# Second layer of an edge network: half of its features in three fp32r products, half in fp32, with a new order of VectorE's and ScalarE's units

## The chip, the cores and the metric

The kernel runs on one core of a Trainium2 chip. The metric is the device time of one execution in microseconds (us). TensorE multiplies, VectorE (DVE), ScalarE (ACT) and GpSimd (POOL) work on tiles, and SyncE (SP) issues plain DMAs. The engines run side by side and order themselves by semaphores alone. In the profile PE is TensorE's matmul and PEld its weight load.

## The reference

```python
h = jnp.maximum(_layernorm(x, axis=-1), 0.0)               # x: 6250 x 256
polarity = jnp.clip(edge_attr[:, 0:1], 0.0, 1.0)           # 206250 edges, sorted by dst
raw = edge_attr[:, 1:]                                     # 64 features
e = jax.nn.relu(raw @ W_e1.T + b_e1) @ W_e2.T + b_e2       # 256 hidden, 256 out
edge_emb = (e * (polarity + 0.01)) @ W_le.T + b_le
msg = jax.nn.relu(h[src] + edge_emb)
aggr = jax.ops.segment_sum(msg, dst, num_segments=6250)
h2 = (h + aggr) @ W_g1.T + b_g1                            # then layer norm, relu, @ W_g2.T + b_g2
out = x + (relu(ln(h2)) @ W_g2.T + b_g2)
```

`W_e2` and `W_le` are multiplied into one 256 x 256 matrix (`wc`) on the chip, since the gate is one number per edge. So an edge costs two layers: 64 to 256 with a ReLU, then 256 to 256.

## The kernel before

The edges are cut into 403 units of 512, each of four blocks of 128. One window of at most 128 nodes takes the messages of seven units (58 windows); the 49 node tiles are brought to their end in between, spread over the units of later windows. A unit u goes through these steps, and each engine runs its own loop over u, in the order written in its block:

- GpSimd gathers the rows of h for the four blocks (L577), at most four units ahead of `total` and three ahead of the second layer.
- ScalarE rounds the raw features to fp32r (`raw_high`, L422) and VectorE computes the rest that rounding lost (`raw_low`, L427). TensorE's `first_layer` (L798, L799) makes two fp32r products for each half k of the hidden features, into the PSUM banks LA[0] and LA[1].
- ScalarE's `hidden_high` (L588) writes relu of both halves to `hh` in fp32, which frees LA for the next unit.
- ScalarE's `seed` (L593) puts the constant c2 in the four LB banks, two a unit. `second_layer` (L820) adds, for each block, two fp32 products of 256 columns. Each fp32 product shows as two records of the profile, so 16 a unit.
- VectorE's `total` (L675) computes gate * LB + gathered row, once a block, ScalarE's `message_high` (L600) rounds its relu to fp32r, and VectorE's `message_low` (L685) computes what is left.
- VectorE's `onehot` (L664) compares slots with an iota; `segment` (L836) multiplies the one-hot rows by high and low parts side by side (512 columns), summing a window in the bank SG[g % 2]: left half the high parts, right half the low.
- After the window's last unit ScalarE's `window_out` (L608) copies all 512 columns to `agw`, TensorE's `window_turn` (L844) transposes and adds both halves by four fp32 products with the identity (eight records), and VectorE's `window_add` (L699) adds the result to `aggT`.

The loops before the change run per unit: TensorE second_layer(u), first_layer(u+2), segment(u-1), then window and node work. ScalarE hidden_high(u+1), lift, raw_high(u+3), seed(u+1), two message_high(u), window_out. VectorE node steps and total(u), message_low(u), raw_low(u+3), onehot(u+1), more node steps. The node steps are `up` (L855, L856), `stats` (L704), `moments` (L708), `invert` (L712), `norm` (L718), `turn` (L863), `lift` (L621), `down` (L869, L870) and `finish` (L725).

Of the kernel before, what the change touches and what calls it, by code (L numbers as in the profile page):

```python
# [4 lines left out]
F32 = mybir.dt.float32  # L5
# [8 lines left out]
D = 256  # L14
# [12 lines left out]
GU = 7  # L27
# [23 lines left out]
def gnn(nc, x, src, dst, src_m, dst_m, pol_m, pol, first, attrT, attr_m, W_e1T, b_e1, b_e1r, W_e2, b_e2, W_leT, b_le,  # L51
        W_g1T, b_g1, ln_g, ln_b, W_g2T, b_g2, out):
    ctx = ExitStack()
    with ctx:
# [15 lines left out]
        w1r = sb("w1r", [P, 2, D], F32R)  # L70
        c2r = sb("c2r", [P, D], F32R)
# [22 lines left out]
        def setup(c):  # L94
# [90 lines left out]
            def vector(eng):  # L185
# [18 lines left out]
                link(eng, eng.tensor_copy(c2r[0:1, :], c2[0:1, :]))  # L204
                eng.tensor_tensor(c2r[32:33, :], c2[0:1, :], c2r[0:1, :].bitcast(F32),
# [259 lines left out]
        def edge_path():  # L465
            with ExitStack() as c:
# [6 lines left out]
                hh = sb("hh", [P, 2, 2, 512], F32, c)  # L473
# [3 lines left out]
                agw = sb("agw", [P, 2 * D], F32, c)  # L477
# [4 lines left out]
                r_hh = sem("r_hh", c)  # L482
                r_l2 = sem("r_l2", c)
# [6 lines left out]
                r_ev = sem("r_ev", c)  # L490
                n_x = [sem(f"n_x{i}", c) for i in range(NXT)]
# [90 lines left out]
                def _(eng):  # L582
                    def hidden_high(u):
                        if u >= 2:
                            eng.wait_ge(r_l2, 2 * (u - 2) + 2)
                        for k in range(2):
                            eng.wait_ge(r_l1, 2 * u + k + 1)
                            eng.activation(hh[:, u % 2, k, :], LA[k][:, :], ACT.Relu).then_inc(r_hh, 1)  # L588
# [15 lines left out]
                    def window_out(g):  # L604
                        eng.wait_ge(r_sg, min(GU * g + GU, UNITS))
                        if g >= 1:
                            eng.wait_ge(r_tr, g)
                        eng.copy(agw[:, :], SG[g % 2][:, :]).then_inc(r_ev, 1)  # L608
# [26 lines left out]
                    for u in range(UNITS):  # L635
                        if u + 1 < UNITS:
                            hidden_high(u + 1)
# [3 lines left out]
                        if u + 3 < UNITS:  # L641
                            raw_high(eng, u + 3)
# [17 lines left out]
                def _(eng):  # L660
                    def onehot(u):
# [18 lines left out]
                    def message_low(u):  # L680
                        if u >= 2:
                            eng.wait_ge(r_sg, u - 1)
                        for q in range(2):
# [5 lines left out]
                                                     op0=ALU.max, op1=ALU.subtract).then_inc(r_ml, 1)  # L689

# [52 lines left out]
                    raw_low(eng, 2)  # L743
                    eng.wait_ge(s_sl, 1)
                    onehot(0)
                    for u in range(UNITS):
                        t = TILE_AFTER.get(u // GU - 1)
                        if u % GU == 4 and t is not None:
                            stats(t)
# [9 lines left out]
                        if u + 3 < UNITS:  # L759
                            raw_low(eng, u + 3)  # L760
                        if u + 1 < UNITS:
                            onehot(u + 1)
# [9 lines left out]
                    moments(NT - 3)  # L772
                    window_add(GROUPS - 1)
# [13 lines left out]
                def _(eng):  # L787
                    c2w = c2r[:, :].rearrange("p (a n) -> p a n", a=1).broadcast_to([P, 2, D])

                    def first_layer(u):  # L790
# [4 lines left out]
                        for k in range(2):  # L795
                            if u >= 1:
                                eng.wait_ge(r_hh, 2 * (u - 1) + k + 1)
# [4 lines left out]
                    def second_layer(u):  # L802

                        eng.wait_ge(r_hh, 2 * u + 2)
# [4 lines left out]
                        for q in range(2):  # L809
# [420 lines left out]
```

## Time and profile before

| | |
|---|---|
| median of 3 runs | 2523.25 us (2518.17 to 2527.77) |
| the profiled execution | 2523.43 us, span 2521.7 us |
| PE busy | 2375.0 us, 94% |
| PEld busy | 1999.1 us, 79% |
| DVE busy | 1885.6 us, 75% |
| ACT busy | 1602.5 us, 64% |
| POOL busy | 1672.9 us, 66% |
| DMA | 138 GB/s on average |
| TensorE's granted clock | 0.99 of full speed on average |

Matmul ends are modelled, and matmuls overlap, so starts are what to compare. The idle time of an engine is put down to what released it, as far as semaphore events tell; "remote" is a releaser that the profile can't name.

### The profile page before, as it was taken

How to read it: one execution, taken by the hardware profiler on the slowest of the kernel's cores; microseconds unless marked ns; L12 is line 12 of the kernel's file. 1: busy time of each engine (PE TensorE's matmuls, PEld its weight loads, DVE VectorE, ACT ScalarE, POOL GpSimd, SP SyncE). 2: the span in 40 equal slices, each digit the busy share in tenths (PEclk: the TensorE clock that was granted, in tenths of full speed). 3: DMA queues.
4: the chain of work that ended last, by engine and by line, in shares of the span. 5: the costliest groups of instructions: out<-in, count | busy, mean ns of one | idle time of the engine just before them, and what ended most of it. 6: DMA issues, size and time to landing. Idle time of an engine off the chain costs nothing.

```text
span 2521.7 us, 35558 instructions
## 1 busy us (share of the span) xinstructions
PE 2375.0 (94%) x10840; PEld 1999.1 (79%) x10840; DVE 1885.6 (75%) x3689; ACT 1602.5 (64%) x3112; POOL 1672.9 (66%) x1679
## 2 busy tenths in 40 slices
PE   5799999999999999999999999999999999999998
PEld 4677888778888788878787888787888788887786
DVE  7686777777777777777777777777777777777775
ACT  7566666666666666666666666666666666666664
POOL 6666666666666666666666666666666666666663
PEclk9899999999999999999999999999999999999999
DMA  9444444444444444444444444444444444444442
GB/s 311 129 135 130 132 138 141 136 128 135 138 141 139 129 140 138 140 132 134 134 146 130 136 132 142 135 142 130 137 140 138 134 135 136 144 131 135 134 142 62
DMA packets 136343, 349.09 MB, mean 138 GB/s; under 512 B 32018, under 2 KB 58324, under 8 KB 136148
## 3 DMA queue, kind: packets, MB, share of 16 engines
q0 software_dynamic: 77376, 211.39, 28.9%
q1 hardware_dynamic: 58772, 135.37, 15.8%
q8 instruction: 89, 1.46, 0.2%
q14 instruction: 106, 0.87, 0.1%
HBM read 333.82 MB, written 12.82 MB: 137 GB/s over the span
## 4 chain that ended last, share of the span: by engine, by line
PE 38%; DVE 28%; another core or an unknown queue 14%; issue 13%; ACT 4%; POOL 1%; DVEq 1%; DMA 1%; ACTq 0%; SPq 0%; POOLq 0%
PE bank L820 23%; DVE bank L675 12%; PE bank L836 6%; DVE oh L664 5%; DVE rlo L427 5%; DVE mhl L685 5%; PE bank L798 3%; PE bank L799 3%; ACT mhl L600 2%; PE bank L844 1%; PE bank L870 1%; POOL x_sba L371 1%; DVEq L692 1%; ACT hh L588 1%
## 5 line engine op out<-in xcount | busy, mean ns | idle before, releaser
L577 POOL DMA_INDIRECT hx<-gather_table,sidx x1612 | 1634.0, 1014 | 802.8 <-issue 430.7
L820 PE MATMUL bank<-wc,hh 128*128 128x256 f32 x6448 | 1465.4, 380 | 1.9 <-issue 1.8
L820 PEld LDWEIGHTS bank<-wc,hh 128*128 128x128 f32 x6448 | 1219.1, 191 | 177.6 <-issue 6.5
L675 DVE SCALAR_TENSOR_TENSOR bank<-bank,gt,hx 128x256 f32<-128x256 f32 x1612 | 683.8, 485 | 521.7 <-remote 389.0
L600 ACT ACTIVATE mhl<-bank 128x512 fp32r<-128x512 f32 x806 | 481.7, 599 | 785.4 <-DVE bank L675 612.2
L685 DVE SCALAR_TENSOR_TENSOR mhl<-bank,mhl 128x512 fp32r<-128x512 f32 x806 | 549.5, 689 | 38.7 <-ACT mhl L600 13.4
L798 PE MATMUL bank<-rhi,w1r 128*128 128x512 f32 x806 | 388.5, 482 | 92.5 <-DVE rlo L427 72.6
L588 ACT ACTIVATE hh<-bank 128x512 f32<-128x512 f32 x806 | 442.0, 600 | 52.1 <-remote 41.3
L593 ACT COPY bank<-c 128x512 f32<-128x512 f32 x802 | 453.9, 613 | 0.0
L836 PE MATMUL bank<-mhl,oh 128*128 128x512 f32 x1612 | 444.2, 397 | 0.9 <-DVE mhl L685 0.5
L836 PEld LDWEIGHTS bank<-mhl,oh 128*128 128x128 f32 x1612 | 305.9, 190 | 73.3 <-DVE mhl L685 0.9
L799 PE MATMUL bank<-rlo,w1r 128*128 128x512 f32 x806 | 319.4, 396 | 0.0
L664 DVE TENSOR_TENSOR oh<-iota,slot 128x512 fp32r<-128x512 f32 x403 | 279.9, 694 | 12.3
L427 DVE TENSOR_TENSOR rlo<-raw,rhi 64x512 fp32r<-64x512 f32 x403 | 278.9, 692 | 12.4
L798 PEld LDWEIGHTS bank<-rhi,w1r 128*128 128x128 f32 x806 | 152.8, 190 | 158.9 <-DVE rlo L427 110.7
L422 ACT CAST rhi<-raw 128x512 fp32r<-128x512 f32 x403 | 254.1, 631 | 0.0
L799 PEld LDWEIGHTS bank<-rlo,w1r 128*128 128x128 f32 x806 | 153.5, 190 | 24.5
L621 ACT ACTIVATE rt<-bank,lnb,lng 128x128 f32<-128x128 f32 x98 | 40.1, 468 | 44.6 <-remote 39.9
L844 PEld LDWEIGHTS bank<-ident,agw 128*128 128x128 f32 x464 | 61.1, 192 | 6.4 <-ACT agw L608 1.1
L844 PE MATMUL bank<-ident,agw 128*128 128x128 f32 x464 | 61.5, 276 | 0.7 <-ACT agw L608 0.7
L870 PE MATMUL bank<-wg,rt 128*128 128x256 f32 x196 | 52.3, 391 | 0.0
L856 PE MATMUL bank<-wg,aggT 128*128 128x256 f32 x196 | 51.8, 388 | 0.0
(92 smaller groups left out, 488.6 us busy)
## 6 DMA issues: line engine op xcount, KB each, us to landing
raw<-in_attr_m SPq DMA_DIRECT2D x202, 512.0 KB
hx<-gather_table,sidx POOLq DMA_INDIRECT x1612
x_sba<-in_x SPq DMA_DIRECT2D x12, 512.0 KB, 8.8
gather_table<-x_sba SPq DMA_DIRECT2D x12, 512.0 KB, 7.9
xt<-in_x SPq DMA_DIRECT2D x48, 128.0 KB
out<-xt SPq DMA_DIRECT2D x48, 128.0 KB
dst_i<-in_dst_m SPq DMA_DIRECT2D x1, 805.5 KB
sidx<-in_src_m SPq DMA_DIRECT2D x1, 805.5 KB
```

The source lines that it names most:

```text
L427: eng.tensor_tensor(rlo[F:P, u % NM, :], part(u)[F:P], rhi[F:P, u % NM, :].bitcast(F32), ALU.subtract).then_inc(r_rl, 1)
L577: eng.indirect_dma_start(out=hx[:, u % NX, j, :], out_offset=None, in_=tables, in_offset=bass.IndirectOffsetOnAxis(ap=sidx[:, t:t + 1], ax ...
L588: eng.activation(hh[:, u % 2, k, :], LA[k][:, :], ACT.Relu).then_inc(r_hh, 1)
L593: eng.copy(LB[(2 * u + q) % 4][:, :].rearrange("p (j n) -> p j n", j=2), c2[:, :].rearrange("p (a n) -> p a n", a=1).broadcast_to([P, 2, D ...
L600: eng.activation(mh[:, u % 2, 2 * q:2 * q + 2, :], LB[(2 * u + q) % 4][:, :].rearrange("p (j n) -> p j n", j=2), ACT.Relu).then_inc(r_mh, 1)
L664: eng.tensor_tensor(oh[:, u % 3, :, :], iota[:, :].rearrange("p (a n) -> p a n", a=1).broadcast_to([P, 4, P]), slot[:, 4 * u:4 * u + 4].re ...
L675: last = eng.scalar_tensor_tensor(out=b, in0=b, scalar=gt[:, t:t + 1], in1=hx[:, u % NX, 2 * q + j, :], op0=ALU.mult, op1=ALU.add)
L685: eng.scalar_tensor_tensor(out=ml[:, u % 2, 2 * q:2 * q + 2, :], in0=LB[(2 * u + q) % 4][:, :].rearrange("p (j n) -> p j n", j=2), scalar=0.0,
L798: eng.matmul(LA[k][:, :], w1r[:, 0, k * P:k * P + P], rhi[:, u % NM, :], start=True, stop=False)
L799: eng.matmul(LA[k][:, :], w1r[:, 1, k * P:k * P + P], rlo[:, u % NM, :], start=False, stop=True).then_inc(r_l1, 1)
L820: last = eng.matmul(o, hh[:, u % 2, k, e0:e0 + P], wc[:, k, :], start=False, stop=(j == 1 and k == 1), skip_group_check=seeded)
L836: last = eng.matmul(SG[g % 2][:, :].rearrange("p (i n) -> p i n", i=2), oh[:, u % 3, j, :], mhl[:, u % 2, j, :, :], start=(u % GU == 0 and ...
```

## The change

Half k = 0 of the hidden features is kept as a rounded part `hh` and a remainder `hl`, both fp32r, and the weights of that half as `wcr[:, 0]` (rounded) and `wcr[:, 1]` (remainder). Its product is hh*wcr0 + hh*wcr1 + hl*wcr0. Half k = 1 stays one fp32 product, from `hf`. `hidden_low` is a new VectorE operation that makes `hl` from LA[0]. So a block has three fp32r products and one fp32 product instead of two fp32 products.

On ScalarE raw_high(u+3) comes first in a unit. On VectorE raw_low(u+3), onehot(u+1) and hidden_low(u+1) come first, ahead of total(u). first_layer(u+1) may write LA[0] when `hidden_low` has read it, and LA[1] when `hf` is written.

For a window ScalarE copies only the right half (256 columns) to one of two buffers, VectorE's new `window_join` adds the left half to it, and `window_turn` is two transposes.

```diff
@@ hidden_high (ScalarE), hidden_low (VectorE, new)
-                        for k in range(2):
-                            eng.wait_ge(r_l1, 2 * u + k + 1)
-                            eng.activation(hh[:, u % 2, k, :], LA[k][:, :], ACT.Relu).then_inc(r_hh, 1)
+                        eng.wait_ge(r_l1, 2 * u + 1)
+                        eng.activation(hh[:, u % 2, :], LA[0][:, :], ACT.Relu).then_inc(r_hh, 1)
+                        eng.wait_ge(r_l1, 2 * u + 2)
+                        eng.activation(hf[:, u % 2, :], LA[1][:, :], ACT.Relu).then_inc(r_hf, 1)
+                    def hidden_low(u):
+                        if u >= 2:
+                            eng.wait_ge(r_l2, 2 * (u - 2) + 2)
+                        eng.wait_ge(r_hh, u + 1)
+                        eng.scalar_tensor_tensor(out=hl[:, u % 2, :], in0=LA[0][:, :], scalar=0.0,
+                                                 in1=hh[:, u % 2, :].bitcast(F32),
+                                                 op0=ALU.max, op1=ALU.subtract).then_inc(r_hl, 1)
@@ window_out (ScalarE), window_join (VectorE, new), window_turn (TensorE)
-                        if g >= 1:
-                            eng.wait_ge(r_tr, g)
-                        eng.copy(agw[:, :], SG[g % 2][:, :]).then_inc(r_ev, 1)
+                        if g >= 2:
+                            eng.wait_ge(r_tr, g - 1)
+                        eng.copy(agw[:, g % 2, :], SG[g % 2][:, D:2 * D]).then_inc(r_ev, 1)
+                    def window_join(g):
+                        eng.wait_ge(r_ev, g + 1)
+                        eng.tensor_tensor(agw[:, g % 2, :], SG[g % 2][:, 0:D], agw[:, g % 2, :], ALU.add).then_inc(r_es, 1)
-                        eng.wait_ge(r_ev, g + 1)
+                        eng.wait_ge(r_es, g + 1)
                         for k in range(2):
-                            for i in range(2):
-                                last = eng.matmul(SG[g % 2][:, D + k * P:D + k * P + P],
-                                                  agw[:, i * D + k * P:i * D + k * P + P], ident[:, :],
-                                                  start=(i == 0), stop=(i == 1))
+                            last = eng.transpose(SG[g % 2][:, D + k * P:D + k * P + P], agw[:, g % 2, k * P:k * P + P], ident[:, :])
@@ ScalarE's loop
                     for u in range(UNITS):
+                        if u + 3 < UNITS:
+                            raw_high(eng, u + 3)
                         if u + 1 < UNITS:
                             hidden_high(u + 1)
...
-                        if u + 3 < UNITS:
-                            raw_high(eng, u + 3)
@@ VectorE's loop
                         t = TILE_AFTER.get(u // GU - 1)
+                        if u + 3 < UNITS:
+                            raw_low(eng, u + 3)
+                        if u + 1 < UNITS:
+                            onehot(u + 1)
+                            hidden_low(u + 1)
...
                         message_low(u)
-                        if u + 3 < UNITS:
-                            raw_low(eng, u + 3)
-                        if u + 1 < UNITS:
-                            onehot(u + 1)
+                        if u % GU == 0 and u >= GU:
+                            window_join(u // GU - 1)
@@ first_layer and second_layer (TensorE)
-                                eng.wait_ge(r_hh, 2 * (u - 1) + k + 1)
+                                eng.wait_ge(r_hf if k else r_hl, u)
...
-                        eng.wait_ge(r_hh, 2 * u + 2)
+                        eng.wait_ge(r_hl, u + 1)
+                        eng.wait_ge(r_hf, u + 1)
...
-                                for k in range(2):
-                                    last = eng.matmul(o, hh[:, u % 2, k, e0:e0 + P], wc[:, k, :],
-                                                      start=False, stop=(j == 1 and k == 1), skip_group_check=seeded)
+                                eng.matmul(o, hh[:, u % 2, e0:e0 + P], wcr[:, 0, :], start=False, stop=False, ...)
+                                eng.matmul(o, hh[:, u % 2, e0:e0 + P], wcr[:, 1, :], start=False, stop=False, ...)
+                                eng.matmul(o, hl[:, u % 2, e0:e0 + P], wcr[:, 0, :], start=False, stop=False, ...)
+                                last = eng.matmul(o, hf[:, u % 2, e0:e0 + P], wc[:, 1, :], start=False, stop=(j == 1), ...)
```

At the start two operations on VectorE make `wcr` from `wc`, and in the tail `window_join` of the last window stands ahead of its `window_add`.

## Rows read from the trace of the kernel before

**Rows 1.** The page's head: span, and busy time of each engine.
```profile
span 2521.7 us, 35558 instructions
PE 2375.0 (94%) x10840; PEld 1999.1 (79%) x10840; DVE 1885.6 (75%) x3689; ACT 1602.5 (64%) x3112; POOL 1672.9 (66%) x1679
```

**Rows 2.** Line L820's own view: durations in ns, first and last start.
```profile
L820 PE MATMUL bank<-wc,hh x6448: 376/379/634, 53.0 to 2498.0; 128*128 128x256 f32 x196
```

**Rows 3.** Timeline of PE: start, length in us, line; one undisturbed unit.
```profile
1116.42 3.61 PE L820 MATMUL bank<-wc,hh 128*128 128x256 f32 x16
1120.11 0.39 PE L799 MATMUL bank<-rlo,w1r 128*128 128x512 f32 x1
1120.34 0.40 PE L798 MATMUL bank<-rhi,w1r 128*128 128x512 f32 x1
...
1121.73 3.61 PE L820 MATMUL bank<-wc,hh 128*128 128x256 f32 x16
```

**Rows 4.** Timeline of PE: a downward node product, and a window's turn.
```profile
1208.41 0.28 PE L869 MATMUL bank<-g2r,onr 128*128 128x256 f32 x1
1208.53 1.03 PE L870 MATMUL bank<-wg,rt 128*128 128x256 f32 x4
1209.39 3.62 PE L820 MATMUL bank<-wc,hh 128*128 128x256 f32 x16
...
1137.06 1.05 PE L844 MATMUL bank<-ident,agw 128*128 128x128 f32 x8
```

**Rows 5.** Timeline of DVE: a cycle in which it doesn't wait.
```profile
1116.71 1.40 DVE L685 SCALAR_TENSOR_TENSOR mhl<-bank,mhl 128x512 fp32r<-128x512 f32 x2
1118.14 0.69 DVE L427 TENSOR_TENSOR rlo<-raw,rhi 64x512 fp32r<-64x512 f32 x1
1118.86 0.69 DVE L664 TENSOR_TENSOR oh<-iota,slot 128x512 fp32r<-128x512 f32 x1
1119.47 1.66 DVE L675 SCALAR_TENSOR_TENSOR bank<-bank,gt,hx 128x256 f32<-128x256 f32 x4
1121.15 1.40 DVE L685 SCALAR_TENSOR_TENSOR mhl<-bank,mhl 128x512 fp32r<-128x512 f32 x2
```

**Rows 6.** Groups by line and form: DVE's node work; busy us, mean ns.
```profile
L718 DVE TENSOR_SCALAR hn<-bank,mv,rs 128x256 f32<-128x256 f32 x49 | 26.7, 544 | 1.8
L699 DVE TENSOR_TENSOR aggT<-aggT,bank 128x256 f32 x58 | 24.1, 415 | 2.6 <-PE bank L844 2.6
L704 DVE BATCH_NORM_STATS2 st<-bank 128x6 f32<-128x256 f32 x49 | 20.9, 426 | 22.7 <-remote 19.2 <-PE bank L856 3.5
L725 DVE TENSOR_TENSOR xt<-bank,xt 128x256 f32<-128x256 f32 x48 | 19.9, 416 | 2.1 <-PE bank L870 2.1
L708 DVE BATCH_NORM_AGGREGATE mv<-st 128x2 f32<-128x6 f32 x49 | 8.5, 173 | 0.1
L712 DVE RECIPROCAL rs<-rs 128x1 f32<-128x1 f32 x49 | 7.6, 155 | 0.0
```

**Rows 7.** The same view: weight loads of the second layer, and `message_low`.
```profile
L820 PEld LDWEIGHTS bank<-wc,hh 128*128 128x128 f32 x6448 | 1219.1, 191 | 177.6 <-issue 6.5
L685 DVE SCALAR_TENSOR_TENSOR mhl<-bank,mhl 128x512 fp32r<-128x512 f32 x806 | 549.5, 689 | 38.7 <-ACT mhl L600 13.4 <-issue 1.1 <-PE bank L836 0.4
```

**Rows 8.** Waits: who waited for whom, us in total, times, longest.
```profile
DVE bank L675 <- remote: 389.0, 132, 8.9
DVE bank L675 <- PE bank L820: 123.0, 86, 5.9
PE bank L798 <- DVE rlo L427: 72.6, 75, 7.2
```

**Rows 9.** Timeline of ACT: the two hidden copies of a unit.
```profile
1136.55 1.08 ACT L588 ACTIVATE hh<-bank 128x512 f32<-128x512 f32 x2
```

**Rows 10.** Timelines of DVE and PE: the stall behind 1121.73.
```profile
1129.85 1.67 DVE L675 SCALAR_TENSOR_TENSOR bank<-bank,gt,hx 128x256 f32<-128x256 f32 x4 [5.86 <-PE bank L820]
1133.71 0.80 PE L798 MATMUL bank<-rhi,w1r 128*128 128x512 f32 x1 [3.05 <-ACT hh L588]
```

More of the change, by code:

```diff
@@ L70, in gnn @@
         w1r = sb("w1r", [P, 2, D], F32R)
+        wcr = sb("wcr", [P, 2, D], F32R)
         c2r = sb("c2r", [P, D], F32R)
@@ L203, in vector @@
                 yield
-                link(eng, eng.tensor_copy(c2r[0:1, :], c2[0:1, :]))
-                eng.tensor_tensor(c2r[32:33, :], c2[0:1, :], c2r[0:1, :].bitcast(F32),
+                eng.tensor_copy(c2r[0:1, :], c2[0:1, :])
+                link(eng, eng.tensor_copy(wcr[:, 0, :], wc[:, 0, :]))
+                eng.tensor_tensor(c2r[32:33, :], c2[0:1, :], c2r[0:1, :].bitcast(F32), ALU.subtract)
+                eng.tensor_tensor(wcr[:, 1, :], wc[:, 0, :], wcr[:, 0, :].bitcast(F32),
                                   ALU.subtract).then_inc(s_wt, 1)
@@ L472, in edge_path @@
                     b = nodes(c, "a", s_o1, s_oa, 0, cx)
-                hh = sb("hh", [P, 2, 2, 512], F32, c)
+                hh = sb("hh", [P, 2, 512], F32R, c)
+                hl = sb("hl", [P, 2, 512], F32R, c)
+                hf = sb("hf", [P, 2, 512], F32, c)
                 oh = sb("oh", [P, 3, 4, P], F32R, c)
@@ L476, in edge_path @@
                 sb("apart", [P, D], F32, c)
-                agw = sb("agw", [P, 2 * D], F32, c)
+                agw = sb("agw", [P, 2, D], F32, c)
                 hn = sb("hn", [P, 2, D], F32, c)
@@ L482, in edge_path @@
                 r_hh = sem("r_hh", c)
+                r_hf = sem("r_hf", c)
+                r_hl = sem("r_hl", c)
                 r_l2 = sem("r_l2", c)
@@ L490, in edge_path @@
                 r_ev = sem("r_ev", c)
+                r_es = sem("r_es", c)
                 n_x = [sem(f"n_x{i}", c) for i in range(NXT)]
@@ L743, in _ @@
                     raw_low(eng, 2)
+                    hidden_low(0)
                     eng.wait_ge(s_sl, 1)
@@ L772, in _ @@
                     moments(NT - 3)
+                    window_join(GROUPS - 1)
                     window_add(GROUPS - 1)
@@ L818, in second_layer @@
                                 e0 = (2 * q + j) * P
-                                for k in range(2):
-                                    last = eng.matmul(o, hh[:, u % 2, k, e0:e0 + P], wc[:, k, :],
-                                                      start=False, stop=(j == 1 and k == 1), skip_group_check=seeded)
+                                eng.matmul(o, hh[:, u % 2, e0:e0 + P], wcr[:, 0, :], start=False, stop=False,
+                                           skip_group_check=seeded)
+                                eng.matmul(o, hh[:, u % 2, e0:e0 + P], wcr[:, 1, :], start=False, stop=False,
+                                           skip_group_check=seeded)
+                                eng.matmul(o, hl[:, u % 2, e0:e0 + P], wcr[:, 0, :], start=False, stop=False,
+                                           skip_group_check=seeded)
+                                last = eng.matmul(o, hf[:, u % 2, e0:e0 + P], wc[:, 1, :],
+                                                  start=False, stop=(j == 1), skip_group_check=seeded)
                             last.then_inc(r_l2, 1)
```

## The prediction

> **What bounds the kernel now.** I read the page's head first, for what the engines have to do, then one undisturbed stretch of TensorE and VectorE in the timeline, then the waits. TensorE is busy 94% of the span and VectorE 75% [rows 1], but a busy share of modelled, overlapping matmuls is no bound, so I count start to start. All second-layer records lie between 53.0 and 2498.0 us [rows 2]: 2445 us for 403 units, and 78 us of the profiled execution's 2523.4 us lie outside them (set-up, first nodes, last nodes). That execution is within 0.2 us of the median, so no correction is made.
>
> TensorE's unit without a stall is 5.31 us from one second layer to the next [rows 3]. Its 16 fp32 records start (3.62 - 0.38) / 15 = 0.216 us apart; a 128-edge block has four of them, 0.864 us. Node work comes on top. An upward or downward product group takes 0.98 us (1208.41 to 1209.39) [rows 4], 49 of each; the eight 128-wide records of a window's turn start (1.05 - 0.28) / 7 = 0.11 us apart, 0.88 us [rows 4], 58 times; a node tile's turn is two such, 0.22 us. Together 49 x 2.18 + 58 x 0.88 = 158 us. 403 x 5.31 = 2140, and 158, make 2298 us; 2445 - 2298 = 147 us are stalls. So TensorE's stream sets 94% of the loop, and its stalls the rest.
>
> VectorE's own cycle, where it doesn't wait, is 4.44 us, from L685 at 1116.71 to L685 at 1121.15 [rows 5]: two of L685, L427, L664, four of L675. Its node work is 24.1 + 26.7 + 20.9 + 19.9 + 8.5 + 7.6 = 108 us in all [rows 6], 0.27 a unit. It needs 4.71 us of the 6.07 that a unit takes on average. 1.36 us a unit are its slack now, and it is this slack that the change spends.
>
> **The change part by part.**
>
> *Second layer.* Of the two fp32 products of a block, one becomes three fp32r products of the same 256 columns. fp32 keeps 2 x 0.216 us. A 256-wide fp32r record with a weight load behind it is in the trace once a node group: L869 at 1208.41, the next record at 1208.53, 0.12 us [rows 4]. Two such behind one another the trace doesn't show. From below the price is half of the 0.216 step of an fp32 record of the same width, 0.108; from above it is 0.19, the length of a weight load's record [rows 7], if loads could not overlap at all. The eight records of L844, each with a load of 0.192 us, start 0.11 apart, which speaks against that end. I take 0.12, the nearest row. A block is then 3 x 0.12 + 0.432 = 0.792 us, 0.072 less; times 1612 blocks, 116 us less of TensorE (174 less at 0.108; at 0.19 it would be 222 us more than now).
>
> Here a rule of the Trainium skill speaks for a larger gain: TensorE: Matmul & The Clock Gate, section Back-to-back issue gap, gives a stream of loads and matmuls 81 ns a matmul at 128 columns and 131 ns at 512. An estimate halfway, 106 ns, would make the saving 183 us. The 512-wide first-layer and segment records here step by about 0.23 us [rows 3], not 0.131, so this trace doesn't bear the rule out and I don't use it.
>
> *Window's turn.* Eight records become two transposes: 6 x 0.11 x 58 = 38 us less on TensorE. The sum of the halves moves to VectorE: one 256-wide add from PSUM, 0.415 us like L699 [rows 6], 58 times, 24 us. ScalarE copies 256 instead of 512 columns. TensorE's stream is then 2298 - 116 - 38 = 2144, and with the 78 outside, **2222 us**.
>
> *hidden_low.* New on VectorE, once a unit: a 128x512 scalar_tensor_tensor with PSUM in, fp32r out, the form of L685, 0.689 us [rows 7], at the pitch of L427 to L664 0.72 us [rows 5]. 403 x 0.72 = 290 us on an engine that so far was not the bound. VectorE's packed time: 403 x (4.44 + 0.72) = 2079, and 108 + 24 of node and join, is 2211; with the 78 outside, **2289 us**. That is more than TensorE's 2222. So the bound moves: TensorE gets 154 us shorter, VectorE 314 us longer, and VectorE comes out 67 us above TensorE. The gain can't be more than 2523 - 2289 = 234 us. From below, the busy time alone (1885.6 + 278 + 24 = 2188 us, and some 40 us of idle ends) would be 2228.
>
> *Order.* raw_low(u+3) and onehot(u+1) move from the end of VectorE's unit to the start of it, which in a cycle is the same place after message_low(u-1), with the unit index one higher: the rounded raw halves are ready one unit earlier. TensorE's idle before L798 that ended with L427 (72.6 us in 75 waits [rows 8]) loses its named cause. What is late next in the same place is hidden_low(u+1): first_layer(u+2) overwrites LA[0], which now VectorE reads too and reads third in its unit, after raw_low and onehot. From the end of message_low(u-1), hidden_low(u+1) ends 3 x 0.72 = 2.2 us later. VectorE then does total(u) 1.66 us, and two message_low 1.40 us. In that time TensorE has first layer and segment 1.75 us and second layer, 4 x 0.792 = 3.2 us: 4.95 us against VectorE's 5.16. TensorE arrives at the wait for hidden_low 0.2 us before it is done, unit after unit. That is VectorE's pace, not a stall of its own. On ScalarE raw_high(u+3) is first; it and the two hidden copies are done within some 1.7 us of the last message_high (the two hidden ones 1.08 us [rows 9]), and VectorE wants the first of them after raw_low and onehot, so that is covered by VectorE's own second message_low and those two operations. If that cover goes, raw_low(u+3) waits, and all of VectorE's unit behind it. Without node work in between I cost it at nothing.
>
> *The join's wait.* window_join(g) waits for ScalarE's window_out, and this for the last segment of the window, which TensorE does after second_layer(u) and first_layer(u+2). VectorE ends message_low(u) some 3.1 us after it began total(u); the segment and the copy are done about 2.9 us after (0.92 + 0.93 of matmuls, their 0.39 of drain, 0.35 of copy, each with a little signalling). Queued behind it are raw_low(u+4), onehot and hidden_low, and so TensorE's first layer. Price: nothing to 2 us, 58 times; I take 0.5 us, 28 us.
>
> *Waits of VectorE.* Nothing in the trace shows how much a packed VectorE waits here. TensorE, the pace setter now, loses 147 us in the loop. The other end: VectorE waited 389.0 us for something the profile doesn't name and 123.0 us for L820 [rows 8]; most of this was its slack. I take 110 us, join included: 147 less half of the 72.6 that the order removes. Bounds: 15 us (nearly packed), and 220 us (a little over half of the 389). Forecast: 2289 + 110 = **2399 us**, 5% faster.
>
> **The rivals.** (A) *VectorE packed.* The waits go with the reorder, as TensorE's now wait until VectorE delivers, and no unit needs more than VectorE has. For it: the front of its unit (2.2 us) needs nothing from TensorE's current unit. Against it: the stalls of today lie in more places than L427's. Time 2289 + 15 to 60: 2300 to 2350.
>
> (B) *Half of the nameless waits stay.* 2289 + 170 to 220: 2460 to 2510.
>
> (C) *Slower: late releases meet an engine without slack.* At 1121.73 TensorE began a second layer whose first half is through at about 1123.6, and VectorE's L675 on it started at 1129.85 after 5.86 us of idling; then TensorE's first layer idled 3.05 us for ScalarE's hh [rows 3, 10]. The profile names TensorE as releaser, yet its matmuls had been done, so the release came late for a reason that I can't see. Today VectorE catches such a loss up from 1.36 us of slack a unit. After the change it has none and each such microsecond counts. Were two thirds of the 389 us added, 2289 + 28 + 259 = 2576. It decides against the change from 206 us on, 53% of them. Against it: a TensorE that is held at every first layer runs less far ahead, and a late release of work that VectorE has not come to yet costs nothing; that is argued, no row shows it.
>
> (D) *Weight loads bound.* If a 128x128 load really costs its record, 0.191 us [rows 7], a block's five cost 0.955 us against 0.864: 147 us more, less 38 of the turn, 2523 + 109 = 2632. The Trainium skill, Trainium Kernel Development and Optimization, section Performance Expectations, calls the busy share of LDWEIGHTS a good metric and that of matmuls a bad one. By it today's 79% would rise to (1999 + 308 - 67) / 2399 = 93%, more loads in less time. L844's 0.11 us step with equal loads speaks against (D).
>
> (E) *Much ado, no change*: the waits grow by what the stream loses, 2511 to 2536.
>
> **How the numbers follow.** Forecast, 2350 to 2460 us: 0.55. A: 0.15. B: 0.12. E: 0.05. C: 0.10. D: 0.03. Beyond 0.5%, some 12 us, a measurement of this kernel can tell a change. Faster: 0.55 + 0.15 + 0.12 = 0.82; within 0.5%: 0.05; slower: 0.13. The range takes A, the forecast and B: 2300 to 2510, 0.82 of the chance.
>
> **What would show it.** VectorE should be busy about 2190 us, over 90% of the span, and idle mainly before L675 and the join. TensorE's busy share should fall, its idle standing before the first layer and released by hidden_low. A unit without a stall should be near 5.2 us, paced by VectorE. A block of second layer should take 0.79 us; at 0.95, (D) holds. The wait on L427 should be gone. If VectorE's nameless waits are still over 200 us, (B) or (C) holds. I am wrong if hidden_low takes clearly more than 0.72 us of VectorE's time, or if TensorE still has no waits, which would mean that VectorE's packed time was over-counted.

## The result, and the profile after

The changed kernel ran at 2575.86 us (2574.36 to 2578.05, 4 runs) against 2522.58 us of the kernel before: ratio 1.0214, 95% interval 1.0199 to 1.0228. It is 2.1% slower. The forecast was 2399 us, 5% faster, with a range of 2300 to 2510 us. Rival C named 2576 us.

The head of the page after, to set beside [rows 1]:

```profile
span 2575.6 us, 38949 instructions
## 1 busy us (share of the span) xinstructions
PE 2269.7 (88%) x12104; PEld 1916.6 (74%) x12104; DVE 2149.9 (83%) x4152; ACT 1588.4 (62%) x3112; POOL 1674.8 (65%) x1679
```

TensorE has 105 us less of busy time (the forecast took 154 us from its stream), VectorE 264 us more (302 us forecast), and nobody is over 90% busy in a kernel that got slower. Something makes both wait. The waits, beside [rows 8] (who waited for whom, us in total, times, longest):

```profile
PEld bank L824 <- issue: 367.8, 304, 5.6
POOL hx L585 <- remote: 261.7, 136, 2.5
DVE bank L692 <- remote: 203.0, 139, 2.8
PE bank L824 <- DVE hl L674: 197.5, 172, 5.2
POOL hx L585 <- PE bank L852: 139.6, 93, 3.5
DVE bank L692 <- PE bank L852: 119.5, 109, 6.2
...
PE bank L824 <- DVE rlo L430: 7.1, 2, 6.4
```

L692 is now `total`, L674 `hidden_low`, L824 the first layer, L852 the fp32 product, L585 the gather. TensorE's wait for `raw_low` shrank from 72.6 to 7.1 us, and `hidden_low` took its place with 197.5 us. VectorE waits 203.0 + 119.5 us before `total`, for a second layer that is done, as this stretch shows. First TensorE, then VectorE, then GpSimd (start us, length us, engine, line; idle before and releaser in brackets):

```profile
1206.91 0.36 PE L846 MATMUL bank<-wcr,hh 128*128 128x256 f32 x1
1207.11 0.28 PE L848 MATMUL bank<-wcr,hh 128*128 128x256 f32 x1
1207.23 0.28 PE L850 MATMUL bank<-wcr,hl 128*128 128x256 f32 x1
1207.35 0.59 PE L852 MATMUL bank<-wc,hf 128*128 128x256 f32 x2
1207.59 0.47 PE L846 MATMUL bank<-wcr,hh 128*128 128x256 f32 x1
...
1208.13 0.59 PE L852 MATMUL bank<-wc,hf 128*128 128x256 f32 x2
1208.38 0.47 PE L846 MATMUL bank<-wcr,hh 128*128 128x256 f32 x1
...
1209.16 0.47 PE L846 MATMUL bank<-wcr,hh 128*128 128x256 f32 x1
```

```profile
1207.58 0.68 DVE L674 SCALAR_TENSOR_TENSOR hl<-bank,hh 128x512 fp32r<-128x512 f32 x1
1209.80 1.67 DVE L692 SCALAR_TENSOR_TENSOR bank<-bank,gt,hx 128x256 f32<-128x256 f32 x4 [1.54 <-PE bank L852]
```

```profile
1211.05 0.94 POOL L585 DMA_INDIRECT hx<-gather_table,sidx  x1 [2.56 <-DVE bank L692]
```

The two blocks that `total(u, 0)` needs end at 1208.13 + 0.59 = 1208.72. VectorE was free at 1208.26 and started at 1209.80: the release came 1.08 us late. GpSimd's next gather waits 2.56 us in turn. I took this through the whole loop (from 130 us on): time from the later of VectorE's own last end and the matmul record's end to the start of L675 or L692. In the kernel before that is 447 us, over 0.1 us in 195 halves of a unit of some 800; after the change 287 us, in 226 (a first count, which e1's expectation quotes, had 281). The hand-over from VectorE to ScalarE in the same traces takes 94 to 95 ns at the median and at the 99th percentile.

The wait before `total` is for two things, the second layer and the gathered rows, so either could be what is late. The trace also keeps the times at which semaphores were raised, and they settle it. TensorE's semaphore for the half above was raised at 1209.78, 1.05 us behind its matmul's end, while TensorE had gone on to the next block at its usual pace; VectorE started 0.02 us later. In all 226 late halves after the change, and in 194 of the 195 before it, such an update of TensorE's stands less than 0.06 us ahead of VectorE's start. Nor is it the second layer alone: of the recorded updates of TensorE's first layer, second layer and segment together, 940 of 1785 came over 0.2 us behind their matmul's end in the kernel before, and 700 of 1794 after the change. Of VectorE's and ScalarE's none did in the loop. So TensorE's releases are late, all of them alike, and nobody else's.

Blocks start 0.78 to 0.79 us apart (1207.59, 1208.38, 1209.16). The packed cycle of VectorE is 5.04 us, from L430 to L430 in this stretch, beside [rows 5]:

```profile
1213.46 0.69 DVE L430 TENSOR_TENSOR rlo<-raw,rhi 64x512 fp32r<-64x512 f32 x1
1214.18 0.69 DVE L681 TENSOR_TENSOR oh<-iota,slot 128x512 fp32r<-128x512 f32 x1
1214.79 0.68 DVE L674 SCALAR_TENSOR_TENSOR hl<-bank,hh 128x512 fp32r<-128x512 f32 x1
1215.39 1.66 DVE L692 SCALAR_TENSOR_TENSOR bank<-bank,gt,hx 128x256 f32<-128x256 f32 x4
1217.07 1.40 DVE L702 SCALAR_TENSOR_TENSOR mhl<-bank,mhl 128x512 fp32r<-128x512 f32 x2
1218.50 0.69 DVE L430 TENSOR_TENSOR rlo<-raw,rhi 64x512 fp32r<-64x512 f32 x1
```

So the price of the second layer stands, that of `hidden_low` was 0.12 us a unit too high, and the waits are what missed.

### The profile page after: what moved, and what is told of

It reads as the page before. It is cut to its first block, busy times and chain, and to the rows that moved or that the text cites. A ratio compares the mean times of both kernels' runs of the same rounds, so it can differ in the third digit from the quotient of the medians.

```text
span 2575.6 us, 38949 instructions
## 1 busy us (share of the span) xinstructions
PE 2269.7 (88%) x12104; PEld 1916.6 (74%) x12104; DVE 2149.9 (83%) x4152; ACT 1588.4 (62%) x3112; POOL 1674.8 (65%) x1679
## 4 chain that ended last, share of the span: by engine, by line
DVE 42%; PE 28%; issue 15%; another core or an unknown queue 7%; ACT 5%; DVEq 1%; POOL 1%; DMA 0%; ACTq 0%; SPq 0%
DVE bank L692 14%; DVE mhl L702 10%; PE bank L852 9%; DVE oh L681 6%; DVE hl L674 6%; PE bank L868 5%; ACT mhl L609 4%; DVE rlo L430 3%; PE bank L824 3%; PE bank L825 2%; PE bank L846 2%; PE bank L848 2%; PE bank L850 2%; PE bank L885 1%
## 5 line engine op out<-in xcount | busy, mean ns | idle before, releaser
L585 POOL DMA_INDIRECT hx<-gather_table,sidx x1612 | 1636.4, 1015 | 855.0 <-issue 394.3
L852 PE MATMUL bank<-wc,hf 128*128 128x256 f32 x3224 | 960.9, 379 | 1.2 <-issue 1.2
L692 DVE SCALAR_TENSOR_TENSOR bank<-bank,gt,hx 128x256 f32<-128x256 f32 x1612 | 685.8, 484 | 324.2 <-remote 203.0
L846 PE MATMUL bank<-wcr,hh 128*128 128x256 f32 x1612 | 710.9, 441 | 0.0
L824 PE MATMUL bank<-rhi,w1r 128*128 128x512 f32 x806 | 363.7, 451 | 266.8 <-DVE hl L674 197.5
L852 PEld LDWEIGHTS bank<-wc,hf 128*128 128x128 f32 x3224 | 494.8, 189 | 1.6 <-issue 1.6
L868 PE MATMUL bank<-mhl,oh 128*128 128x512 f32 x1612 | 454.1, 405 | 0.5 <-DVE mhl L702 0.5
L848 PE MATMUL bank<-wcr,hh 128*128 128x256 f32 x1612 | 454.0, 282 | 0.2 <-issue 0.2
L850 PE MATMUL bank<-wcr,hl 128*128 128x256 f32 x1612 | 452.4, 281 | 1.0 <-issue 1.0
L824 PEld LDWEIGHTS bank<-rhi,w1r 128*128 128x128 f32 x806 | 152.8, 190 | 397.7 <-issue 367.8
L846 PEld LDWEIGHTS bank<-wcr,hh 128*128 128x128 f32 x1612 | 307.8, 191 | 45.9 <-issue 0.5
L848 PEld LDWEIGHTS bank<-wcr,hh 128*128 128x128 f32 x1612 | 308.5, 191 | 44.9 <-issue 0.5
L850 PEld LDWEIGHTS bank<-wcr,hl 128*128 128x128 f32 x1612 | 305.6, 190 | 0.5 <-issue 0.5
L430 DVE TENSOR_TENSOR rlo<-raw,rhi 64x512 fp32r<-64x512 f32 x403 | 280.8, 697 | 13.6 <-issue 1.1
L674 DVE SCALAR_TENSOR_TENSOR hl<-bank,hh 128x512 fp32r<-128x512 f32 x403 | 275.5, 684 | 0.0
L425 ACT CAST rhi<-raw 128x512 fp32r<-128x512 f32 x403 | 246.8, 613 | 0.0
```

Of the source, the lines that this page charges most:

```text
L585: eng.indirect_dma_start(out=hx[:, u % NX, j, :], out_offset=None, in_=tables, in_offset=bass.IndirectOffsetOnAxis(ap=sidx[:, t:t + 1], ax ...
L692: last = eng.scalar_tensor_tensor(out=b, in0=b, scalar=gt[:, t:t + 1], in1=hx[:, u % NX, 2 * q + j, :], op0=ALU.mult, op1=ALU.add)
L824: eng.matmul(LA[k][:, :], w1r[:, 0, k * P:k * P + P], rhi[:, u % NM, :], start=True, stop=False)
L846: eng.matmul(o, hh[:, u % 2, e0:e0 + P], wcr[:, 0, :], start=False, stop=False, skip_group_check=seeded)
L848: eng.matmul(o, hh[:, u % 2, e0:e0 + P], wcr[:, 1, :], start=False, stop=False, skip_group_check=seeded)
L850: eng.matmul(o, hl[:, u % 2, e0:e0 + P], wcr[:, 0, :], start=False, stop=False, skip_group_check=seeded)
```

## The experiments

They ran in five sittings (a sitting is a group of kernels that ran one after the other on one chip, with the kernel before among them). The second and the third were on the same chip, the others on three different ones. A finding of its own: the kernel before took 2519, 2373, 2556, 2374 and 2523 us in them, steady within 0.4% in each. I call a sitting near 2373 quiet and one over 2500 disturbed. The result above stands beside a kernel before of 2523 us. Each comparison below names its sitting.

### First sitting, disturbed (before 2519 us): what do the gathers, hidden_low, the order and the window work cost?

**e1, no gathers.**
```diff
-                    for u in range(UNITS):
+                    for u in range(NX):
                         if u >= NX and u % NW == 0:
```


> The changed kernel, but GpSimd gathers only the first four units' rows; later units add those again, so the messages are wrong from unit 4 on and 1596 of 1612 indirect DMAs are gone. In the profile of the changed kernel, 281 us of VectorE's idle before total stand where its own last work was done, the second layer's matmul had ended by its record and the gathered rows had landed: the release came late. Theory 1 (descriptor writing or transfers of the gathers delay TensorE's releases): these waits go, the kernel runs at VectorE's packed time, 2280 to 2330 us. Theory 2 (the lateness is TensorE's own, whatever GpSimd does): 2540 to 2590 us, unexplained waits still over 200 us.

`total` no longer waits for later units' rows either. Measured 2275 us (one run). The page's head and the wait before `total`:

```profile
PE 2206.1 (97%) x12104; PEld 1901.1 (84%) x12104; DVE 2141.0 (94%) x4152; ACT 1592.6 (70%) x3112; POOL 55.3 (2%) x83
...
DVE bank L692 <- PE bank L852: 43.3, 92, 6.1
```

VectorE is 94% busy and "remote" is gone. Theory 1 holds, 5 us under its range: in a disturbed sitting the gathers delay TensorE's releases, and this costs the changed kernel 300 us. The 16 gathers that are left run one after the other from 55.6 to 76.9 us, and 7 of TensorE's updates between 67.9 and 79.6 us are late, by up to 7 us. In the 2.2 ms behind them none is.

**e2, no hidden_low.**
```diff
                     def hidden_low(u):
+                        if u >= 2:
+                            return
...
-                        eng.wait_ge(r_hl, u + 1)
+                        eng.wait_ge(r_hl, min(u + 1, 2))
+                        eng.wait_ge(r_hh, u + 1)
```


> The changed kernel, but hidden_low runs for the first two units only; later units multiply that old remainder, so the product hl*wcr0 is wrong, and VectorE has 401 operations of 0.68 us fewer (273 us of work); TensorE's stream is unchanged. Theory 1 (VectorE has no slack left, and late releases cost in full): back under TensorE's bound of 2222 us plus stalls of about 150 us, 2330 to 2420 us. Theory 2 (the shorter, denser fp32r records of TensorE are themselves what makes the kernel slow): 2520 us or more.

Measured 2525 us (one run), in theory 2's range, but not for its reason, as e1 has the same fp32r records and runs at 2275 us. 273 us less work on VectorE bought 51 us, and the line of `total` shows where the rest went (busy us, mean ns, idle before and releasers):

```profile
L694 DVE SCALAR_TENSOR_TENSOR bank<-bank,gt,hx 128x256 f32<-128x256 f32 x1612 | 683.2, 484 | 481.9 <-remote 303.2 <-PE bank L857 174.5 <-issue 4.1
```

Its idle rose from 324 to 482 us, of which late releases are 477 us by the sum above. What VectorE no longer does, it waits. With TensorE's stream 154 us shorter and VectorE's work nearly as before, the kernel comes out 0.2% above the kernel before. So in a disturbed sitting TensorE's saving is worth nothing, already without VectorE's new work (the new order, 0.7% by e3, is still in e2), and that work costs about 50 us on top. "An engine without slack pays late releases in full" is not enough as a theory: it would have given 2330 to 2420 us. A unit takes 6.07 us on average in the kernel before and in e2, 6.2 to 6.3 in the changed kernel, though TensorE's stream in e2 needs only 5.3 us. That the loop through the late releases has a pace of its own is my reading of this, and isn't shown.

**e3, old order** (raw_low and onehot behind message_low, raw_high behind hidden_high).
```diff
-                        if u + 3 < UNITS:
-                            raw_low(eng, u + 3)
                         if u + 1 < UNITS:
-                            onehot(u + 1)
                             hidden_low(u + 1)
...
                         message_low(u)
+                        if u + 3 < UNITS:
+                            raw_low(eng, u + 3)
+                        if u + 1 < UNITS:
+                            onehot(u + 1)
```


> The changed kernel with the old places of the raw split and one-hot: on ScalarE raw_high(u+3) behind hidden_high(u+1), on VectorE raw_low(u+3) and onehot(u+1) behind message_low(u), and hidden_low(u+1) first in the unit. In a packed cycle this is the same sequence but for hidden_low ahead of raw_low and onehot by one place. Theory 1 (VectorE's total work and the late releases set the time): within 1% of 2576 us. Theory 2 (hidden_low third in the unit is what holds TensorE's first layer, 197.5 us of idle): 2400 to 2500 us, since hidden_low then ends 1.4 us earlier.

2557.6 us, ratio to before 1.0149 (1.0132 to 1.0166). Against the changed kernel's ratios (1.0214 here, 1.0217 and 1.0222 below) the new order costs 0.7%. TensorE's idle for hidden_low is 169.3 us against 197.5. Theory 1, in the main. The changed kernel itself didn't run in this sitting, so the comparison goes through the ratios.

**e4, old window work** (512 columns copied, eight records, no join).
```diff
-                        eng.copy(agw[:, g % 2, :], SG[g % 2][:, D:2 * D]).then_inc(r_ev, 1)
+                        eng.copy(agw[:, :], SG[g % 2][:, :]).then_inc(r_ev, 1)
...
-                        if u % GU == 0 and u >= GU:
-                            window_join(u // GU - 1)
```


> The changed kernel with the old window work: ScalarE copies 512 columns, TensorE turns and adds by eight records, no window_join on VectorE. VectorE loses 58 x 0.415 = 24 us of work and the wait for ScalarE's copy, TensorE gets 38 us more. Theory 1 (VectorE is the bound): 20 to 60 us faster, 2515 to 2556 us. Theory 2 (TensorE is the bound): 30 to 40 us slower, 2606 to 2616 us.

2575.9 us (2570 to 2581), ratio 1.023 (1.0204 to 1.0256). No difference from the changed kernel can be told, and neither theory's number came. The window part is worth nothing either way there. In the changed kernel's trace the join waited 1.4 us in all, so my 28 us for it was wrong.

### Second sitting, quiet (before 2373 us)

**e5, the kernel before without gathers** (e1's edit).

> The kernel before, with the gathers of all units but the first four left out, as in e1 (messages wrong from unit 4 on). e1 ran at 2275 us with all of TensorE's releases prompt. Theory 1 (gathers cost each kernel whatever stands above its own packed time): this one runs at TensorE's packed time, 2298 + 78 = 2376 us, so 2370 to 2400, and the changed kernel beats it by about 4 to 5%, the gain that was forecast. Theory 2 (gathers cost only the changed kernel, as it has no slack): 2500 to 2520 us.

2373.5 us, beside 2373.5 us of the kernel before with all its gathers. The time is TensorE's packed 2376 us of the prediction, but the comparison meant for it was gone: here gathers cost nothing.

**e6, plain DMAs from SyncE's queue; e7, plain DMAs from GpSimd's own queue.**
```diff
-                            eng.indirect_dma_start(out=hx[:, u % NX, j, :], out_offset=None, in_=tables,
-                                                   in_offset=bass.IndirectOffsetOnAxis(ap=sidx[:, t:t + 1], axis=0)
-                                                   ).then_inc(r_hx[t % (4 * NX)], 16)
+                            eng.dma_start(hx[:, u % NX, j, :], tables[(t % NT) * P:(t % NT) * P + P, :]).then_inc(r_hx[t % (4 * NX)], 16)
```
(e7's edit; e6 issues the same DMAs in SyncE's block behind each pair of raw loads.)

> The changed kernel with the gathers replaced by plain DMAs of the same size from SyncE's queue (128 consecutive rows of the table instead of the edges' rows, so the messages are wrong). GpSimd writes no descriptors in the loop; the DMA engines move the same bytes. Theory 1 (GpSimd's descriptor writing delays TensorE's releases): 2280 to 2330 us, releases prompt. Theory 2 (the traffic itself delays them): 2500 to 2590 us.

> The changed kernel with each indirect DMA replaced by a plain DMA of 128 consecutive rows that GpSimd issues from its own queue (messages wrong). Descriptors are still written by software, but without indices. Theory 1 (software descriptor writing as such): between 2450 and 2590 us, releases late. Theory 2 (only the indirect form, with its reading of indices, or only random rows): 2280 to 2350 us.

2265 and 2267 us. In a quiet sitting that tells only that the packed time is under 2270 us with the full traffic. e7 was run again below.

**e8, five buffers.**
```diff
-NX = 4
+NX = 5
...
-                        if u >= LEAD:
-                            eng.wait_ge(r_l2, 2 * (u - LEAD) + 2)
```


> The changed kernel with five units of gather buffers instead of four and without GpSimd's wait for second_layer(u-3), so that it waits for total(u-5) alone. Theory 1 (late releases hold GpSimd up too, and the loop of GpSimd, TensorE and VectorE is what costs): gathers run further ahead, GpSimd waits less, but the releases are late while it writes: within 1.5% of 2576 us. Theory 2 (GpSimd's run-ahead is too short, and rows come late): 2350 to 2450 us.

2270.1 us, ratio 0.9565 (0.955 to 0.9581), with every gather in place. The waits:

```profile
POOL hx L583 <- issue: 422.1, 1383, 0.4
POOL hx L583 <- DVE bank L690: 116.2, 228, 0.8
...
DVE bank L690 <- PE bank L850: 38.2, 91, 1.8
```

No "remote" at all, 38 us before `total`. I first took this for a cure. The next sitting showed otherwise.

### Third sitting, disturbed (before 2556 us)

**e9, the changed kernel again.**

> The changed kernel, nothing edited. The kernel before ran at 2519 us beside e1 to e4 and at 2373 us beside e5 to e8, with and without gathers there: the late releases belong to some chips. Theory 1 (they decide the sign): beside a kernel before of about 2373 us this runs at 2265 to 2300 us, ratio 0.955 to 0.97; beside one of about 2520 us at 2560 to 2590 us, ratio 1.015 to 1.025. Theory 2 (the change costs by itself): ratio over 1.0 in either case.

2613.3 us, ratio 1.0217 (1.0193 to 1.0242), inside theory 1's ratio.

**e10, e8's kernel again.**

> The kernel of e8 (five units of gather buffers, no wait of GpSimd for the second layer), which ran at 2270 us beside a kernel before of 2373 us. Theory 1 (the late releases, where there are any, act on VectorE whatever the run-ahead of the gathers): beside a kernel before of 2520 us 2520 to 2600 us, and equal to the changed kernel within 0.5% beside one of 2373 us. Theory 2 (GpSimd's run-ahead is what hurts): 2270 to 2350 us beside 2520 us.

2671.8 us, ratio 1.0459 (1.0439 to 1.0479). The same file that ran at 2270 us, on the same chip. More run-ahead of the gathers is worse here, by 2.2% against e9; whether that is the fifth buffer or the missing wait isn't told apart. VectorE's late-release idle is about the same (314 us, 321 in e9). TensorE's wait for `hidden_low` grew from 237.5 to 273.1 us, and its clock was at the lower of its two levels for 216 us of the loop, beside 130 in e9. Theory 2 is out; theory 1's range was too narrow.

**e11, e7's kernel again.**

> The kernel of e7 (plain DMAs of consecutive rows from GpSimd's queue; messages wrong), 2267 us beside a kernel before of 2373 us. It tells only beside one of 2520 us. Theory 1 (software-written descriptors as such delay TensorE's releases): 2450 to 2590 us there. Theory 2 (only the indirect form): 2270 to 2300 us there.

2267.3 us, as in the quiet sitting. The gather's line and `total`:

```profile
L585 POOL DMA_DIRECT2D hx<-gather_table x1612 | 856.5, 538 | 1322.5 <-PE bank L850 864.7 <-DVE bank L690 419.2 <-issue 35.3
L690 DVE SCALAR_TENSOR_TENSOR bank<-bank,gt,hx 128x256 f32<-128x256 f32 x1612 | 677.1, 482 | 40.2 <-PE bank L850 39.2
```

Same bytes, same queue, same number of DMAs; 538 ns each instead of 1015, and no late release. Theory 1 is out: neither the traffic nor software-issued DMAs as such do it. None of TensorE's updates is over 0.2 us late.

### Fourth sitting, quiet (before 2374 us)

**e12, gathers of near and repeated rows; e13, two gathers a unit.** Their edits stand at e17 and e18.

> The changed kernel, but the gathers take the sorted destinations as indices instead of the sources (messages wrong): the indirect form stays, its rows lie together and repeat. Judged beside a kernel before of over 2500 us. Theory 1 (the indirect form itself delays TensorE's releases): within 1.5% of the changed kernel there, 2540 to 2650 us, releases late. Theory 2 (random rows in memory do): 2265 to 2330 us.

> The changed kernel with two indirect gathers a unit instead of four from unit 4 on (the other two blocks add old rows, messages wrong). No gathers gave 2275 us (e1), four a unit 2576 to 2613 us. Theory 1 (lateness grows with the time in which GpSimd issues gathers): about in the middle or below, 2300 to 2450 us. Theory 2 (a few gathers are as bad as many): over 2500 us.

2268.3 and 2268.0 us: without late releases they can't tell anything, and were run again.

**e14, LEAD = 2.** (`-LEAD = 3`, `+LEAD = 2`)

> The changed kernel with LEAD = 2: GpSimd gathers unit u only when the second layer of u-2 is done, one unit later than now; nothing is left out. The longer run-ahead of e10 made it slower (2672 against 2613 us). Theory 1 (a longer run-ahead lets gathers run back to back and spreads the lateness, so a shorter one helps): 1 to 5% faster than the changed kernel. Theory 2 (rows then come late to total): 2650 us or more.

2269.8 us, ratio 0.956 (0.9544 to 0.9576). It differs from the changed kernel by one unit of run-ahead and leaves nothing out. It is not known what it does in a disturbed sitting.

**e15, the kernel before with e7's plain DMAs.**

> The kernel before with plain DMAs of consecutive rows from GpSimd's queue in place of the gathers (messages wrong), as e11 for the changed one (2267 us). Theory 1 (without late releases each kernel runs at its bound): 2370 to 2380 us, so the change is worth 4.5% there. Theory 2 (the changed kernel's plain-DMA time is low for another reason): under 2300 us or over 2450 us.

2374.8 us, theory 1. With e7's 2267 us: where releases come in time, the second layer and all that goes with it are worth 4.5%.

### Fifth sitting, disturbed (before 2523 us)

**e16, the changed kernel a third time.**

> The changed kernel, nothing edited, a third time. Theory 1 (the sign hangs on the late releases): beside a kernel before of about 2374 us 2265 to 2285 us, ratio 0.953 to 0.965; beside one of over 2500 us ratio 1.015 to 1.03. Theory 2 (the change costs by itself): ratio over 1.0 beside 2374 us.

2579.8 us, ratio 1.0222 (1.0205 to 1.0239).

**e17, gathers of near and repeated rows.**
```diff
-                (sidx[:, 0:FULL], src_m), (sidx[0:TAIL, FULL:TILES], src[FULL * P:E][:, None]),
+                (sidx[:, 0:FULL], dst_m), (sidx[0:TAIL, FULL:TILES], dst[FULL * P:E][:, None]),
```


> The kernel of e12 (sorted destinations as indices, messages wrong). It tells only beside a kernel before of over 2500 us. Theory 1 (the indirect form delays the releases): within 1.5% of the changed kernel in the same sitting. Theory 2 (random rows do): 2265 to 2330 us.

2576.3 us, within 0.2% of e16, waits alike:

```profile
L692 DVE SCALAR_TENSOR_TENSOR bank<-bank,gt,hx 128x256 f32<-128x256 f32 x1612 | 684.8, 483 | 320.1 <-remote 193.6 <-PE bank L852 125.4 <-issue 1.1
```

Theory 1: random rows in memory are not the cause.

**e18, two gathers a unit.**
```diff
-                        for j in range(4):
+                        for j in range(4 if u < NX else 2):
```


> The kernel of e13 (two gathers a unit instead of four, messages wrong). It tells only beside a kernel before of over 2500 us. Theory 1 (lateness grows with the time in which GpSimd issues gathers): 2300 to 2450 us. Theory 2 (a few are as bad as many): over 2500 us.

(`total` of the other two blocks doesn't wait for new rows.) 2276.9 us, under theory 1's range: half of the gathers don't cost half, but next to nothing (2268 us for the same file in a quiet sitting).

```profile
L585 POOL DMA_INDIRECT hx<-gather_table,sidx x814 | 774.3, 951 | 1414.6 <-DVE bank L692 693.2 <-PE bank L852 575.5 <-issue 140.0
L692 DVE SCALAR_TENSOR_TENSOR bank<-bank,gt,hx 128x256 f32<-128x256 f32 x1612 | 677.7, 483 | 49.1 <-PE bank L852 37.4 <-remote 7.5 <-issue 2.9
```

GpSimd then rests 1415 us, and of VectorE's nameless waits two are left, 7.5 us. All 8 late updates of TensorE's lie before 80 us, where four gathers a unit still run one after the other.

So the indirect form alone isn't enough either. The disturbed runs with late releases all through have GpSimd at work for some 1640 us (1015 ns a gather, four a unit); those without, for 774 us (e18, indirect) and 857 us (e11, plain). Whether the form counts, or the time for which GpSimd is at it in a unit, is not told apart: eight plain DMAs a unit in a disturbed sitting would be the test, and weren't run.

## Why the prediction was wrong

The step that failed is the term "Waits of VectorE", 110 us with an upper bound of 220: in the measured sitting it was 2576 - 2289 = 287 us over the sum, for a cause that the sum took as slack. Part by part:

*The bound before.* Right for quiet sittings: 2298 + 78 = 2376 us packed, 2373 measured (e5 and the kernel before beside it). The 147 us that I booked as TensorE's stalls are the disturbance itself: 2523 - 2373 = 150. I read them as stalls that any pace setter has, with L427 named for half, and that is the first error: in e5's quiet run TensorE waits 4.8 us for L427, not 72.6. The kernel before had 447 us of late-release idle on VectorE, of which its slack hid two thirds.

*Second layer.* 0.792 us a block forecast, 0.78 to 0.79 measured. Rival D, loads that don't overlap, is out: five loads of 0.19 us fit in 0.785. The 106 ns a 256-wide matmul that the prediction estimated from the Trainium skill's two figures (TensorE: Matmul & The Clock Gate, section Back-to-back issue gap) isn't borne out either, as L848, L850 and L852 start 0.12 us apart. The busy share of weight loads, which (D) put at 93%, fell to 74%.

*hidden_low.* 0.72 us of pitch forecast; the cycle went from 4.44 to 5.04, so 0.60. Its start overlaps the end of onehot (1214.79, with onehot at 1214.18 + 0.69) and its end the start of total.

*VectorE becomes the bound, 2289 us.* Held wherever releases are prompt: 2265 (e6), 2267 (e7, e11), 2268 (e12, e13), 2270 (e8, e14) and, in disturbed sittings, 2275 (e1) and 2277 (e18). 12 to 24 us under the sum, which the 0.12 us of hidden_low's pitch (48 us) more than covers. All are then 94 to 95% VectorE.

*Order.* The forecast had it at nothing, with TensorE's wait moved from L427 to hidden_low. (Its 1.75 us for first layer and segment should be 5.31 - 16 x 0.216 = 1.85 us, which leaves TensorE 0.1 us ahead of VectorE, not 0.2; no sum uses it.) The wait moved (72.6 to 7.1, and 197.5 us new); the price in a disturbed sitting is 0.7% (e3).

*The join's wait.* 28 us forecast, 1.4 us in the trace.

*Waits of VectorE: 110 us, bounds 15 and 220.* This is the step that failed. It was 324 us before `total` in the changed kernel. The bound of 220 was drawn from half of the 389 us, on the argument that most of it was slack, and the forecast added to it as if the late releases were a constant of the kernel. In quiet sittings the term is 36 to 39 us, near its lower bound.

*Rival C* had the sign, the mechanism in the main and, by luck of two thirds, the number: 2289 + 287 = 2576. That the late releases decide the sign, e1 and e11 show. Yet e2 shows that its reason, no slack on VectorE, is the smaller part: without hidden_low VectorE has its slack back, and the kernel gains 51 us where 155 to 245 were expected. What the late releases do to the loop as a whole is more than their sum on one engine. Its counter-argument, that a held TensorE would cost less by late releases, is half true: with 197.5 us of holding there were 226 late halves against 195, but they came to 287 us against 447.

*The clock* adds to it. The mean granted clock fell from 0.990 to 0.979 (e9: 0.969, e10: 0.952; e8, the same file as e10, 0.994). After a hold of 2.18 us on hidden_low the array ran at the lower of its levels, 1.2 GHz, the first layer's step being 0.42 us instead of 0.23:

```profile
1203.28 0.68 PE L824 MATMUL bank<-rhi,w1r 128*128 128x512 f32 x1 [2.18 <-DVE hl L674]
1203.77 0.63 PE L825 MATMUL bank<-rlo,w1r 128*128 128x512 f32 x1
1204.19 0.63 PE L824 MATMUL bank<-rhi,w1r 128*128 128x512 f32 x1
1204.62 0.63 PE L825 MATMUL bank<-rlo,w1r 128*128 128x512 f32 x1
```

Summed over the loop (from 130 us on) the lower level was granted for 77 us, against 28 us before. Work at half rate loses half of its time, so this explains 25 us at most of the 53.

*What stays open.* What differs between quiet and disturbed sittings I can't tell; the same file ran at 2270 and 2672 us. It isn't which chip: these two were the same one, some twenty minutes apart, though e9's expectation still laid it to some chips. In the disturbed traces with gathers part of all engines' semaphore records is missing (221 of TensorE's 2015 in the changed kernel, and some in e18), while the quiet traces and e11's have them all. Every execution here was recorded, so whether the recording has a part in it can't be told. How an indirect DMA keeps TensorE's releases back is not shown; a fixed delay per DMA isn't it, as two a unit cost nothing. The changed kernel itself was never run in a quiet sitting: that it would run at about 2270 us follows from e8, e12 and e14, which ran there and differ from it in buffers, indices or one unit of run-ahead, but wasn't measured. No version was found that is faster than the kernel before in both kinds of sitting.

## What to carry to other kernels

An idle row whose releaser had long been done is not slack and not noise: sum it apart from the rest, and ask what else runs at that time, before work is moved onto the engine that shows it. When a bound engine has neighbours at 75% and stalls that nobody explains, a shorter stream on it can be worth nothing, and a cheap test is to leave out the suspected transfers once in the kernel before (e5's kernel was meant for that, but wasn't run in a disturbed sitting). Where a wait is for two things, the times at which the semaphores were raised tell which of them is late. Keep the kernel before in every group of runs: one and the same file ran 18% slower in one sitting than in another.

## What the runs showed of the hardware

Two things I had not expected. With four indirect DMAs of GpSimd's a unit, TensorE's semaphore updates can come a microsecond and more behind the end of their matmuls while TensorE goes on with the next ones (287 us of VectorE's idle over 226 cases in the changed kernel, 1.3 us each, 447 us over 195 before, 2.3 us each). Plain DMAs of the same bytes from the same queue don't do this (e11: none late), and two indirect ones a unit hardly do (e18: 8 updates, all before 80 us). Updates of VectorE's and ScalarE's aren't touched: none in the loop is over 0.2 us late. And this comes and goes between sittings, on one and the same chip too: 2373 against 2519 to 2556 us for the kernel before, each steady within 0.4%; in the quiet ones none of TensorE's updates is late, with all gathers in place (e8, e14).
